# The product of keys and decay factor formed by VectorE instead of GpSimd, in a 1-core Trainium2 kernel

## The reference, cut to what matters

```python
q, k, v = silu(x @ Wq), silu(x @ Wk), silu(x @ Wv)
log_f = log_sigmoid(x @ Wf1 @ Wf2); beta = sigmoid(x @ Wbeta) * 2.0
k = l2norm(k); k_ = -beta[..., None] * k
gk = interleave(log_f, zero)
a = interleave(k_ * exp(log_f), k_); bb = interleave(k, k)
kk = interleave(zero, k); vv = interleave(zero, v); qq = interleave(zero, q)
def step(S, (g, a_t, b_t, k_t, v_t, q_t)):
    bS = einsum('bhk,bhkv->bhv', b_t, S)
    S = exp(g)[..., None] * S + a_t[..., None] * bS[:, :, None, :] + k_t[..., None] * v_t[:, :, None, :]
    o = einsum('bhk,bhkv->bhv', q_t, S)
```

## Time and profile before

| | us |
|---|---|
| Three runs, median | 1864.21 (1859.53 to 1866.02) |
| Profiled execution, its own time | 1851.54 |
| Its span, first to last instruction | 1849.6 |
| Busy in the span: PE / VectorE / ScalarE / GpSimd | 1583.3 / 1113.3 / 786.7 / 767.4 |
| Mean granted clock of TensorE | 0.935 |

### The profile page before, as it was taken

How to read it: one execution, slowest core, us unless ns; L and a number is a source line. 1 busy time by engine, 2 the same in 40 slices (tenths; PEclk the granted TensorE clock), 3 DMA queues, 4 the chain that set the end, 5 groups by cost and what they waited for, 6 DMA issues and landing times. The chain is left out here.

```text
span 1849.6 us, 68392 instructions
## 1 busy us (share of the span) xinstructions
PE 1583.3 (86%) x26476; PEld 1286.8 (70%) x26477; DVE 1113.3 (60%) x3370; ACT 786.7 (43%) x1829; POOL 767.4 (41%) x986
## 2 busy tenths in 40 slices
PE   5499999999577978878887888977886999999994
PEld 4499999999435565455654556535564999999994
DVE  7646444443457886787868878588773556444441
ACT  2143333333266444673447734476332443333331
POOL 2554522222145552646527466183651235422222
PEclk9999999999788999798998889978997999999997
DMA  9563432322300200002000020000102833332324
GB/s 301 174 201 70 93 48 46 51 46 48 78 3 8 68 26 23 4 7 70 23 23 5 9 67 23 23 5 7 46 23 94 253 78 75 74 64 46 51 46 114
DMA packets 84239, 116.28 MB, mean 63 GB/s; under 512 B 12952, under 2 KB 74464, under 8 KB 82016
## 3 DMA queue, kind: packets, MB, share of 16 engines
q1 hardware_dynamic: 56160, 74.17, 13.2%
q0 software_dynamic: 27360, 37.80, 11.7%
q10 hardware_dynamic: 608, 2.96, 0.5%
HBM read 64.87 MB, written 54.21 MB: 64 GB/s over the span
## 5 line engine op out<-in xcount | busy, mean ns | idle before, releaser
L1069 POOL DMA_INDIRECT x<-ffn_yout,ffn_place x142 | 222.0, 1563 | 532.5 <-DVE ffn_yout L1001 455.3
L1007 DVE TENSOR_TENSOR ffn_inner<-ffn_inner,ffn_bank 128x512 f32<-128x512 f32 x142 | 97.5, 687 | 343.1 <-PE ffn_bank L877 338.5
L958 ACT ACTIVATE ffn_inner<-ffn_bank 128x512 f32<-128x512 f32 x142 | 84.8, 597 | 458.9 <-PE ffn_bank L877 458.9
L877 PE MATMUL ffn_bank<-ffn_tileT,ffn_gate_now 128*128 128x128 f32 x2272 | 280.0, 277 | 0.0
L877 PE MATMUL ffn_bank<-ffn_tileT,ffn_up_now 128*128 128x128 f32 x2272 | 277.5, 275 | 0.0
L887 PE MATMUL ffn_bank<-ffn_w,ffn_inner 128*128 x1136 | 268.9, 380 | 1.8 <-DVE ffn_yout L1001 1.8
L877 PEld LDWEIGHTS ffn_bank<-ffn_tileT,ffn_gate_now 128*128 128x128 f32 x2272 | 268.2, 194 | 0.1
L877 PEld LDWEIGHTS ffn_bank<-ffn_tileT,ffn_up_now 128*128 128x128 f32 x2272 | 265.8, 192 | 0.0
L887 PEld LDWEIGHTS ffn_bank<-ffn_w,ffn_inner 128*128 128x128 f32 x1136 | 205.0, 191 | 24.5 <-issue 2.5
L820 ACT COPY ffn_gate_now<-ffn_w 128x1024 f32 x142 | 148.4, 1045 | 29.4 <-issue 21.9
L820 DVE COPY ffn_up_now<-ffn_w 128x1024 f32 x142 | 99.4, 700 | 59.5 <-issue 47.8
(11 more groups left out here) (614 smaller groups left out, 3141.4 us busy)
## 6 DMA issues: line engine op xcount, KB each, us to landing
ffn_w<-in_w1t_dram SPq DMA_DIRECT2D x16, 1024.0 KB, 5.4
ffn_tile<-xs SPq DMA_DIRECT2D x122, 130.0 KB, 2.1
ffn_w<-in_w2t_dram SPq DMA_DIRECT2D x16, 512.0 KB, 6.7
at_a_sb<-x SPq DMA_DIRECT2D x32, 256.0 KB, 2.8
ffn_x<-in_x_dram SPq DMA_DIRECT2D x16, 256.0 KB, 5.0
x<-ffn_x SPq DMA_DIRECT2D x16, 256.0 KB, 6.4
x<-at_a_sb SPq DMA_DIRECT2D x16, 256.0 KB, 2.1
xs<-ffn_empty SPq DMA_DIRECT2D x23, 130.0 KB, 3.0
```

What stands on the lines that cost most here:

```text
L877: t = pe.matmul(bank[:, i * P:(i + 1) * P], half_now[half][b][:, k, i * P:(i + 1) * P], rowsT[b][:, k * P:(k + 1) * P], start=(k == 0), st ...
L958: act.activation(inner[b][:, :], p_g[b][:, :], ACT.Silu).then_inc(s_silu, 1)
L1007: dve.tensor_tensor(inner[b][:, :], inner[b][:, :], p_u[b][:, :], ALU.mult).then_inc(s_act, 1)
L1069: pool.indirect_dma_start(total, bass.IndirectOffsetOnAxis(ap=place[b][:, 0:1], axis=0), yout[b][:, :], None, compute_op=ALU.add).then_inc ...
```

## The change

The product kf = k x fd leaves GpSimd's `gpsimd(n)` and enters VectorE's `differences(n)`, between its three subtractions into `d` and the one into `ek`. It is written into one of two planes (n even, n odd) that lie in one tensor in front of the planes of k; the first of the two is the last plane of v, which is not in use in this stage. VectorE forms kf(n) once the factor is there (`s_f`, a wait that stood in that place before) and, from chain 2, once GpSimd has finished chain n - 2 (`s_pr`, new), since that chain read the same plane. GpSimd now waits for VectorE's `s_kf` where it waited for its own before. The access pattern that reads kf and k of the chain together gets another offset and stride.

```diff
--- before.py
+++ after.py
@@ -1136,9 +1136,9 @@
         epsk, eps4 = last("epsk", [P, 1]), last("eps4", [P, 1])
         mask = last("mask", [P, UN * GS])
 
-        v, gt = (last(n, [P, CHAINS, PT]) for n in ("v", "gt"))
-        kfk = last("kfk", [P, 1 + CHAINS, PT])
-        kf, k = kfk[:, 0, :], kfk[:, 1:1 + CHAINS, :]
+        gt = last("gt", [P, CHAINS, PT])
+        kfk = last("vkk", [P, 2 * CHAINS + 1, PT])
+        v, kf, k = kfk[:, 0:CHAINS, :], kfk[:, CHAINS - 1:CHAINS + 1, :], kfk[:, CHAINS + 1:2 * CHAINS + 1, :]
         qb = last("qb", [P, 2, CHAINS, PT])
         kb, q = qb[:, 0, :, :], qb[:, 1, :, :]
 
@@ -1982,6 +1982,9 @@
             dve.tensor_tensor(level(d[b], l).rearrange("p (u m) x -> p u m x", u=UN),
                               around(gx[b], T, 0, 1), around(gs[b][:, :, :], T, T, 0), ALU.subtract)
         dve.wait_ge(s_f, n + 1)
+        if n >= 2:
+            dve.wait_ge(s_pr, n - 1)
+        dve.tensor_tensor(kf[:, b, :], k[:, c, :], fd[n % 4][:, :], ALU.mult).then_inc(s_kf, 1)
         dve.tensor_tensor(ek[:, c, :].rearrange("p (u s) -> p u s", s=GS),
                           gs[b][:, :, CT:GS].to_broadcast([P, UN, GS]), gx[b], ALU.subtract).then_inc(s_d, 1)
 
@@ -2024,16 +2027,15 @@
         b, c = n % 2, chain(n)
         out = prod[b][:, :].rearrange("p (n x) -> p n x", x=FE // 8)
         f2 = fd[n % 4][:, :].rearrange("p (n r) -> p n r", r=2)
-        kf2 = kf.rearrange("p (n r) -> p n r", r=2)
+        kf2 = kf[:, b, :].rearrange("p (n r) -> p n r", r=2)
         both = qb[:, :, c, :].rearrange("p a (n r) -> p n a r", r=2)
         late2 = late[:, :, :].rearrange("p a n -> p n a")
         NB = PT // 2
 
         def planes(inner):
-            return bass.AP(tensor=kfk, offset=0, ap=[[(1 + CHAINS) * PT, P], [2, NB]] + inner + [[(1 + c) * PT, 2]])
+            return bass.AP(tensor=kfk, offset=(CHAINS - 1 + b) * PT, ap=[[(2 * CHAINS + 1) * PT, P], [2, NB]] + inner + [[(2 + c - b) * PT, 2]])
 
         pool.wait_ge(s_f, n + 1)
-        pool.tensor_tensor(kf, k[:, c, :], fd[n % 4][:, :], ALU.mult).then_inc(s_kf, 1)
         pool.tensor_tensor(late[:, :, :], qb[:, :, c, :].rearrange("p a (n r) -> p a n r", r=2)[:, :, :, 1],
                            f2[:, :, 1].unsqueeze(1).to_broadcast([P, 2, NB]), ALU.mult).then_inc(s_lt, 1)
         if n >= 2:
```

## The result

The kernel after the change took 1870.62 us (median of 6 runs, 1866.17 to 1879.97), the kernel before, beside it, 1863.32 (median of 6, 1859.53 to 1866.02): ratio 1.005, with an interval of 1.0027 to 1.0073. So the change costs 7.3 us by the difference of the medians and 9.3 by the ratio of the runs, with an interval of 5.0 to 13.6 us. The forecast was 1871, of which 6.6 us were the change.

The account below looks back on a forecast made before the run. The loop VectorE, ScalarE, PE was taken as the bound, GpSimd nearly level. Per pass 2.2, 1.3, 1.7 and 1.4 us, together 6.6, on the median 1864.2 gave 1871 us; range 1858 to 1882.

Parts of the forecast that it names:

- The bound: In the changed stage: the loop VectorE, ScalarE, PE sets the pace, 10.70 us per pair of chains; GpSimd, 11.46, nearly level.
- Which products lie on the path: VectorE's new products: chains 0, 1, 2, 4, 6 count; 3, 5, 7 are hidden by its waits for PE.
- No stall at the reuse of a plane: VectorE's new wait for GpSimd's chain n - 2: that chain ends 3 us or more before, so nothing stalls.
- The rival in which GpSimd was the bound: GpSimd's chains set the stage's end, so moving products off gains: up to 22 us, 1842, or half, 1853; chance 0.12.
- Mostly absorbed: Rival: further products on VectorE's path fit in small gaps, 0 to 5 us slower, 1867; chance 0.30.
- The port at every time: Rival: all five path products meet a GpSimd instruction, 3.7 us per pass, 15 in all, 1879; chance 0.13.
- What is added: On VectorE's path: five products of 0.34 us, 1.7 us per pass, plus the port's meetings.
- The port: VectorE's product meeting GpSimd: 0.4 us at chain 2, 0.6 more at chain 0 in the first pass; chains 1, 4, 6 free.
- What is taken off: GpSimd's relief in the first pass's tail, and slack in later passes: 0.5, 0.8, 0.4 and 0.7 us.
- The wait at keys(2): VectorE's wait, 3.40 us in the last pass: some 1.4 us accumulated delay may vanish in it, half taken off.
- GpSimd's busy time: In the changed profile: GpSimd busy 25 us less, VectorE 13 to 20 us more.
- The pair: Two chains in the second pass: 11.0 to 11.1 us instead of 10.70.

Follow-up runs that it names:

- experiment 1: Changed kernel with only the products of chains 3, 5 and 7 on VectorE, the others left on GpSimd: 1860.47 us, 0.9995 of before.
- even chains (2): Changed kernel with only the products of chains 2, 4 and 6 on VectorE: 1867.58 us, 1.004 of before.
- experiment 3: Kernel before without the products of chains 1 to 7 of each pass, chain 0's reused: 1858.09 us, 0.9982 of before.
- experiment 4: Kernel before, the product also formed on VectorE into an unread plane, GpSimd's kept: 1866.68 us, 1.0038 of before.
- experiment 9: The changed kernel again, unaltered, on another chip: 1864.08 us, 1.0065 of before.
- experiment 5: Changed kernel, VectorE's product taking a PSUM operand in place of the factor in SBUF: 1864.31 us, 1.0018 of before.
- loop shortened (7): Kernel before with decay(5) and decay(7) moved into VectorE's waits for PE in keys(2) and keys(4): 1860.31 us, 0.9997 of before.
- experiment 8: Kernel before with decay(5) and decay(7) moved into VectorE's waits and the products of chains 3 and 7 on VectorE: 1855.65 us, 0.9978 of before.

## Why the prediction was right, and where its terms were off

**Right.** The bound: the loop VectorE, ScalarE, PE, with GpSimd beside it (experiments 1 to 3). Which products lie on the path: chains 3, 5 and 7 cost nothing, chains 2, 4 and 6 cost 6.6 us (forecast for these three: 4 x (1.02 + 0.4) = 5.7). No stall at the reuse of a plane. GpSimd waits for the new product in 24 of 32 chains, and this is free (experiment 4). PE's sums of the last chain no longer wait for GpSimd: what is left in the list of waits is the sums of chain 0 of each pass,

```profile
PE at_bank L2142 <- POOL at_tm L2049: 6.9, 4, 3.6
```

against 8.5 us, 6 times, before. The rival in which GpSimd was the bound (0.12) is refuted by experiment 3. "Mostly absorbed" (0.30, 0 to 5 us) is refuted by experiment 9, whose interval begins at 8.0 us, and by VectorE's steps below; the first comparison alone, with 5.0 us at its low end, would just leave it. The port at every time (0.13, +15 us) lies above both differences of medians, 7.3 and 10.9, but the upper ends of the intervals, 13.6 and 16.1, come near or reach it. What speaks against it is the rows: 7 of 32 products meet nothing, and those of chains 4 and 6 lose 0.12 to 0.18 us, not 0.4.

**Off in size, and partly lucky.** The predicted time, 1871, met the measured 1870.62 better than its terms did. The median of before came out at 1863.32 and not 1864.21, and the change at 7.3 us by the medians, 9.3 by the ratio, and 10.9 and 12.0 in experiment 9, where 6.6 were forecast.

Which terms were off is read from the steps between the starts of VectorE's top-level products (`left_top`, one per chain). A step that holds no wait for PE's top level is VectorE's own work: from the stage's start to keys(0) and on to keys(1), and from keys(2), keys(4) and keys(6) to the one behind. The other three steps end with a wait for PE, and the end runs from keys(7) to the memset. Against the one profile of before, in us over all four passes:

| kernel | VectorE's own steps | step to keys(2) | steps to keys(4) and keys(6) | end | sum |
|---|---|---|---|---|---|
| after | +9.2 | +1.4 | 0.0 | -1.4 | +9.2 |
| after again (9) | +9.1 | +3.5 | 0.0 | -1.3 | +11.3 |
| odd chains (1) | 0.0 | +4.9 | -0.6 | -1.0 | +3.3 |
| even chains (2) | +7.1 | +3.7 | +0.4 | -1.4 | +9.8 |
| no product (3) | -0.1 | +2.4 | -0.2 | -1.3 | +0.8 |
| both engines (4) | +9.3 | +2.0 | -0.6 | -1.1 | +9.6 |
| PSUM operand (5) | +6.1 | +3.1 | +0.5 | -1.3 | +8.4 |
| loop shortened (7) | -5.3 | -0.6 | 0.0 | +7.6 | +1.6 |

VectorE's own steps repeat within 0.1 us. The step to keys(2) does not: it is longer than in before's profile even in experiment 3, where VectorE does nothing more. So its part of a stage's growth is not shown to be the change's.

- *What is added: 1.7 per pass and the port, 9.0 us in all.* VectorE's steps grew by 9.2. Within it two terms err against each other. The products themselves cost 6.1 us (experiment 5) for the 6.8 taken: the two in front of keys(0) add only 0.55 us together, because the product of the keys that met GpSimd there before now takes 1.53 us and not 1.65. The meetings cost the other 3.1, where 2.2 were taken.
- *The port, 0.4 per pass and 0.6 in the first.* The step that failed is "GpSimd has mostly run out of work and waits for this very product, so its port is free". It holds for chains 0 and 1, but for chain 0 of the first pass. At chains 4 and 6 GpSimd had just been released by ScalarE's factor, and the product met its k x q: 0.56 and 0.54 us for 0.42. With 0.36 at chain 2 that is some 0.64 us per pass on the path, and about 0.4 to 0.5 more at chain 0 of the first pass.
- *What is taken off: 0.5, 0.8, 0.4 and 0.7 us, 2.4 in all.* The ends of the stage are shorter by 1.1, 0.3, 0.0 and 0.0 us. The first pass gave more than was taken, the slack in the other passes nearly nothing. The first pass's 1.1 is not GpSimd's relief alone: in experiment 4, where nothing leaves GpSimd but keys(7) come later, its end is 1.0 us shorter too. In the last pass the end is 9.85 us for 9.84, and VectorE's wait of 3.40 us at keys(2) is not slack: it ends with PE, and PE's own idle stretches inside its tiles, which the trace puts down to no releaser, came along with the delayed work (1.83 and 0.93 us; before 2.12 and 0.86).
- *The wait at keys(2), taken as unchanged.* It is what the profiles disagree on. Of the 1.88 us by which the first pass differs between the two profiles of after, 1.85 lie in it (first profile above, second below, each with PE's tiles of a half top level). In the second PE's granted clock was 0.50 all through 552.0 to 560.8, its lower level of 1.2 GHz, against 0.88 over 560.0 to 566.7 in the first; it also had idle stretches of 0.77 and 1.13 us without a releaser. What starts these stretches stays open.

```profile
562.11 0.85 PE L2132 MATMUL at_bank<-pass_right_top,pass_left_top 32*32 32x48 f32 x63
566.68 0.42 DVE L2003 TENSOR_TENSOR pass_left_top<-at_vkk,at_wide 128x256 f32<-128x256 f32 x1 [1.09 <-PE at_bank L2132]
...
556.88 1.50 PE L2132 MATMUL at_bank<-pass_right_top,pass_left_top 32*32 32x48 f32 x63
560.82 0.42 DVE L2003 TENSOR_TENSOR pass_left_top<-at_vkk,at_wide 128x256 f32<-128x256 f32 x1 [2.92 <-PE at_bank L2132]
```

- *GpSimd's busy time.* Forecast 25 us less, it fell by 19.3. The 32 products did hold it for 24.7 us, but two neighbours grew. One is k x q, by 1.1 us (23.8 to 24.9, the meetings with the new product; 23.4 in experiment 5). The other is `late`, by 2.05 (27.00 to 29.05): it is now the first of the chain and takes over, at chain 1 of each pass, a meeting with VectorE's product of the keys (1.31 to 1.32 us for 0.85) that the old product had there in three passes (1.18 to 1.19 us). It grows as much in experiment 5. VectorE's +18.2 lies in its forecast of 13 to 20, but "0.41 us for most" is wrong: 7 of 32 took that.
- *The pair.* 11.0 to 11.1 forecast, 11.17 and 11.54 measured: 0.15 of it is the meeting at chains 4 and 6, and 0.37, once, PE's lower clock.

## What to carry to other kernels

An engine that is busy without a gap is not yet the bound: ask whose wait ends last with it. The same three instructions cost 0 us where VectorE waits for PE behind them and 6.6 us where it doesn't, so place moved work in such a wait, chain by chain if need be, rather than everywhere. And where two limits lie close, each edit alone shows nothing or a loss; only the two together (experiment 8) moved the time.

## What the runs showed of the hardware

Two things had been expected otherwise. A VectorE product of 256 elements with both inputs in SBUF met GpSimd in 25 of 32 cases, although GpSimd has idle time in most chains; what it loses is from 0.12 to 0.51 us and nearly the same at the same chain in every pass (0.77 at chain 2, 0.57 at 3, 0.56 at 4, 0.81 at 5, 0.54 at 6, 0.80 at 7), so it can be read once and multiplied. It is always the rest of GpSimd's instruction less 0.13 us, in the 25 rows of after as in the 10 of experiment 1 that met it. And GpSimd lost less in such a meeting than VectorE: its k x q behind the new product grew from 0.73 to 0.91 us at chains 2 and 3 (784.51, 789.71) and not at all at the others, while a 512-element product of VectorE had made a product of that size 0.45 us longer. The Trainium skill ("SBUF — State Buffer", Who interferes with whom) has the pair of ports as an exclusive lock: the first comer holds it for its whole instruction and fully blocks the second. VectorE's rows agree, 0.13 us apart: it waits out the instruction in flight. With a GpSimd that runs back to back it still comes in behind that one instruction, and in experiment 1 it lost at most 0.69 us (1.10 for 0.41).
